# Gathered neighbour rows: slots filled in order of place, blanked by twos two gathers ahead, and their maximum taken two pairs later

## The chip, the cores and the metric

The kernel runs on one core of one Trainium2 chip. The metric is the device time in microseconds (us), the median of three runs. The core has a matrix engine (PE), a vector engine (DVE), a scalar engine (ACT), a general one (POOL, also called GpSimd) and a queue for transfers (SP). They run their own instruction lists and meet only at semaphores.

## The reference

A graph has N = 4096 nodes with 128 features each, `x`, and an adjacency matrix `adj` of 4096 x 4096 with about 16 ones in each row. Two layers follow one another:

```
neighbour_max[i] = max over j with adj[i, j] != 0 of x[j]      (0 without neighbours)
x1 = layernorm(x + neighbour_max)

h  = x1 @ W
e  = leaky_relu((h @ a_src)[:, None] + (h @ a_dst)[None, :], slope 0.2)
att = softmax(e over the valid neighbours); entries under 1e-4 become 0; times the row's degree
out = layernorm(x1 + elu(h + att @ h))
```

The change is in the first layer, the maximum over neighbours.

## The kernel before

**The first layer** goes over eight groups of 512 rows (four tiles of 128), and in each group over 16 pairs of segments (a segment is 128 columns of `adj`). PE turns the adjacency (`turn`, L1027), ranks its ones (`rank`, L1037), and picks for each row and segment one neighbour by a matrix product with `x` split in three bf16 parts (`select`, L1056). DVE folds each pair's result into a running maximum (`best`, L1457). So one neighbour of each segment is dealt with by PE. ACT evicts between them (L785, L792).

**What PE can't take.** If a row has several neighbours in one segment, the others are found by codes and put on a list. DVE works on the list of group g-1 while group g is being selected: `top_keys` at pairs 0, 1, 3, 5, `decode` at pairs 6 and 7, `make_lists` at pairs 8 and 9. The list has up to 15 entries a row. The first five (`DIRECT`) of every row are gathered straight from `x` by row number; for the rows that have more, ten further gathers (`EXTRA`) fetch rows that are later routed to their place by a matrix product.

**The gathers** are POOL's. `G` has 32 slots of 128 partitions x 128 features. A group uses 30 of them: 20 for direct rows (5 entries x 4 tiles) and 10 for extra ones. A list entry that is empty points out of bounds, and its gather writes nothing; so each slot is first blanked with a very small number. POOL's own list of instructions for one group reads: load quarters 0 and 1 of the next group's adjacency (L647, each waits until PE has turned what stood there), blank slot 0, then gathers 0 to 9, each followed by the blank for the next one, load quarter 2, gathers 10 to 19, load quarter 3, gathers 20 to 29. Gather n waits until blank n is complete (`blanked`). The direct gathers (L704) also wait for `list_ready` from `make_lists` (L1547), the extra ones (L712) for the list of extras that DVE writes at pair 12. The blanks are at L696.

**Who takes the rows.** `direct_max` on DVE waits for all 20 direct gathers of group g-2 and folds 20 slots to 4 in three steps (L1582, L1585, L1589): the first step at pair 2 of group g, the two others at pair 4. `extra_rows` at pair 10 waits for the ten extra gathers and folds them (L1597 to L1604); PE routes the result (`route`, L1092) at pair 11, `aggregate` and `normalise` end the layer at pairs 12 to 15. PE's product `heads` (L1146) stands behind pair 4. The first group whose rows are folded this way inside the loop is group 0, during group 2.

**The end of the first layer** overlaps the second. The second layer runs over parts of 4 to 6 segments in a fixed order (`ORDER`): ACT makes the weights of a part (L873), DVE masks them by the adjacency (L1704), PE multiplies (L1246). ACT and DVE may be up to four parts ahead of PE. What is left of the first layer is done between these parts: `direct_max` of groups 6 and 7 behind parts 2 and 12, `extra_rows` of them at 5 and 14, `make_lists` of group 7 at part 3.

Of the kernel before, what the change touches and what calls it, by code (L numbers as in the profile page):

```python
# [15 lines left out]
GT = 4  # L16
# [53 lines left out]
DIRECT = 5  # L70
# [93 lines left out]
def build(nc, x, adj, W, a, out, adjT, x1_all, h_all, d_all, v_all):  # L164
    with ExitStack() as ctx:
# [473 lines left out]
        @block.gpsimd  # L639
        def _(pool):  # L640
            def load_adj(g, k):

                if g >= GROUPS:
                    return
                if g:
                    pool.wait_ge(turned, (g - 1) * PAIRS + (k + 1) * QPAIRS)
                pool.dma_start(adj_in[:, k, :, :], adj_g[g][:, :, k * QUARTER * SEG:(k + 1) * QUARTER * SEG]  # L647
                               ).then_inc(adj_loaded[k], 16)

            half = QUARTER * SEG // 2  # L650

            def load_first(k):

                c = k * QUARTER * SEG
                pool.dma_start(adj_in[:, k, :, 0:half], adj_g[0][:, :, c:c + half]).then_inc(adj_first[k], 16)

            def load_second(k):
                c = k * QUARTER * SEG
                pool.dma_start(adj_in[:, k, :, half:2 * half], adj_g[0][:, :, c + half:c + 2 * half]
                               ).then_inc(adj_loaded[k], 16)  # L660

            load_first(0)
            pool.iota(before[:, :], [[-1, P]], base=0, channel_multiplier=1,
                      allow_small_or_imprecise_dtypes=True).then_inc(consts_pool, 1)
            pool.iota(part_id[:, :], [[0, 1]], base=0, channel_multiplier=1,
                      allow_small_or_imprecise_dtypes=True).then_inc(consts_pool, 1)
            pool.iota(code_val[:, :], [[-BLOCK, BLOCKS - 1]], base=0, channel_multiplier=1,
                      allow_small_or_imprecise_dtypes=True).then_inc(consts_pool, 1)
            pool.iota(block_id[:, :], [[1, BLOCKS]], base=0, channel_multiplier=0,
                      allow_small_or_imprecise_dtypes=True).then_inc(consts_pool, 1)  # L670
            pool.iota(seg16[:, :, :], [[16, SEGS], [0, BLOCKS]], base=0, channel_multiplier=0,
                      allow_small_or_imprecise_dtypes=True).then_inc(consts_pool, 1)
            pool.iota(place_iota[:, :], [[1, P]], base=1 - P, channel_multiplier=0,
                      allow_small_or_imprecise_dtypes=True).then_inc(consts_pool, 1)
            pool.iota(row_id[:, :], [[P, TILES]], base=0, channel_multiplier=1,
                      allow_small_or_imprecise_dtypes=True).then_inc(consts_pool, 1)
            load_second(0)
            pool.wait_ge(consts_pool, 7)
            pool.memset(xs[96:P, QUARTER:SEGS, :], ABSENT).then_inc(x_blank[1], 1)

            for k in range(1, QUARTERS):
                pool.wait_ge(adj_first[k - 1], 16)
                load_first(k)
                pool.wait_ge(adj_loaded[k - 1], 16)
                load_second(k)

            SLOT_AT = [k * GT + t for t in range(GT) for k in range(DIRECT)] + [DIRECT * GT + k for k in range(EXTRA)]

            def blank(g, n):
                if g and n == 0:
                    pool.wait_ge(direct_read, g)
                if g and n == DIRECT * GT:
                    pool.wait_ge(extra_ready, g)
                pool.memset(G[:, SLOT_AT[n], :], ABSENT).then_inc(blanked, 1)  # L696

            def gather(g, n):
                pool.wait_ge(blanked, g * len(SLOT_AT) + n + 1)
                if n < DIRECT * GT:  # L700
                    t, k = n // DIRECT, n % DIRECT
                    if n == 0:
                        pool.wait_ge(list_ready, g + 1)
                    pool.indirect_dma_start(  # L704
                        out=G[:, SLOT_AT[n], :], out_offset=None, in_=x,
                        in_offset=bass.IndirectOffsetOnAxis(ap=idx[:, t, k:k + 1], axis=0),
                        bounds_check=N - 1, oob_is_err=False).then_inc(gathered, 16)
                else:
                    k = n - DIRECT * GT
                    if k == 0:  # L710
                        wait_taken(pool, "index", g + 1)
                    pool.indirect_dma_start(  # L712
                        out=G[:, SLOT_AT[n], :], out_offset=None, in_=x,
                        in_offset=bass.IndirectOffsetOnAxis(ap=idx_extra[:, k:k + 1], axis=0),
                        bounds_check=N - 1, oob_is_err=False).then_inc(extra_gathered, 16)
                if n + 1 < len(SLOT_AT):
                    blank(g, n + 1)

            for g in range(GROUPS + 1):
                load_adj(g + 1, 0)  # L720
                load_adj(g + 1, 1)
                if g:
                    blank(g - 1, 0)
                    for n in range(DIRECT * GT // 2):
                        gather(g - 1, n)
                load_adj(g + 1, 2)
                if g:
                    for n in range(DIRECT * GT // 2, DIRECT * GT):
                        gather(g - 1, n)
                load_adj(g + 1, 3)  # L730
                if g:
                    for n in range(DIRECT * GT, len(SLOT_AT)):
                        gather(g - 1, n)


            pool.wait_ge(ex_listed, 1)
            for c in range(QUARTERS):
                pool.indirect_dma_start(  # L738
                    out=ex_adj[:, c * QUARTER * SEG:(c + 1) * QUARTER * SEG], out_offset=None,
                    in_=adj_q, in_offset=bass.IndirectOffsetOnAxis(ap=exact_idx[:, c:c + 1], axis=0)).then_inc(ex_loaded[c], 16)  # L740
            pool.wait_ge(ex_listed, 2)
            pool.wait_ge(x1_stored, 16 * GROUPS)
            pool.indirect_dma_start(
                out=ex_x1, out_offset=None, in_=x1_all,
                in_offset=bass.IndirectOffsetOnAxis(ap=exact_idx[:, QUARTERS:QUARTERS + 1], axis=0)).then_inc(ex_rows, 16)

            pool.wait_ge(ex_out_ready, 1)
            pool.wait_ge(out_stored[0], 16 * (GROUPS // 2))
            pool.wait_ge(out_stored[1], 16 * (GROUPS // 2))
            pool.indirect_dma_start(  # L750
                out=out, out_offset=bass.IndirectOffsetOnAxis(ap=exact_idx[:, QUARTERS + 1:QUARTERS + 2], axis=0),
                in_=ex_out, in_offset=None, bounds_check=N - 1, oob_is_err=False).then_inc(ex_stored, 16)
            pool.wait_ge(ex_stored, 16)
# [619 lines left out]
        def _(dve):  # L1373
# [341 lines left out]
            for g in range(GROUPS):  # L1715
                for u in range(PAIRS):
# [3 lines left out]
                    if g >= 1:  # L1720
                        if u in (0, 1, 3, 5):
                            top_keys(g - 1, (u + 1) // 2)
                        if u in (2, 4) and g >= 2:
                            direct_max(g - 2, u // 2 - 1)
                        if u in (6, 7):
                            decode(g - 1, u - 6)
                        if u in (8, 9):
                            make_lists(g - 1, u - 8)
                        if u == 10 and g >= 2:
                            extra_rows(g - 2)  # L1730
                        if u == 11 and g >= 2:
                            take_route(g - 2)
                        if u == 11:
                            place_extras(g - 1)
                        if u == 12 and g >= 2:
                            aggregate(g - 2)
                        if u == 12:
                            list_extras(g - 1)
                            if g >= 2:
                                add_own(g - 2)  # L1740
                        if u == 13 and g >= 2:
                            sums(g - 2)
                        if u == (14 if g < GROUPS - 1 else 5):
                            count(g - 1)
                        if g == GROUPS - 1 and u in (14, 15):
                            mask_piece(0, u - 14)
                        if u == 15 and g >= 2:
                            normalise(g - 2)
# [432 lines left out]
```

## Time and profile before

| | us |
|---|---|
| median of 3 runs | 856.14 (855.97 to 856.28) |
| the profiled execution | 856.39 |
| its span, first to last instruction | 854.6 |
| busy in the span: PE | 681.6 |
| DVE | 581.6 |
| ACT | 579.7 |
| POOL | 359.0 |

One execution was recorded by the hardware profiler. Busy is the time in which an engine executed instructions; issuing a transfer from SP, waiting on a semaphore and branching don't count. The granted clock of PE was 0.896 of full speed over the span. POOL's gathers are shown for the time in which POOL makes their descriptors, not for that of the transfer. The stage of the first layer goes from about 10 to 505 us, the gathers from 92 to 616 us.

### The profile page before, as it was taken

The numbers are of one execution on the slowest core, as the hardware profiler recorded it, in microseconds if no ns is written. First come the engines' busy times: TensorE is split into PE (matmuls) and PEld (weight loads), VectorE is DVE, ScalarE is ACT, GpSimd is POOL, SyncE is SP. The second block draws the span as 40 slices with busy tenths as digits, with TensorE's granted clock in tenths as the row PEclk, the third lists the DMA queues.
The fourth block names the chain that finished last, engine by engine and source line by source line (L and its number), as shares of the span: only waits on it lengthen the run. The fifth ranks groups of instructions, "written<-read, shape, count | busy, mean of one in ns | idle before, by whom it ended". The sixth has DMA issues, their size and how long they took to land.

```text
span 854.6 us, 17555 instructions
## 1 busy us (share of the span) xinstructions
PE 681.6 (80%) x6675; PEld 518.7 (61%) x6675; DVE 581.6 (68%) x1320; ACT 579.7 (68%) x853; POOL 359.0 (42%) x534
## 2 busy tenths in 40 slices
PE   3999976966966967966966859799498989899843
PEld 1656643634634634634644439698398888899842
DVE  4657646836836836836846679883374999999683
ACT  4998773754754754754763787689137999998461
POOL 4100466666666666666566566766500000000020
PEclk9999996987987987987996969999699999999957
DMA  9997353743743843743744142231022122322030
GB/s 191 208 181 150 91 120 59 177 109 84 177 108 82 179 106 82 176 108 81 176 106 102 42 161 66 72 113 39 25 86 76 56 81 81 118 81 57 13 53 15
DMA packets 60513, 87.38 MB, mean 102 GB/s; under 512 B 7714, under 2 KB 33326, under 8 KB 60428
## 3 DMA queue, kind: packets, MB, share of 16 engines
q0 software_dynamic: 27328, 42.14, 27.4%
q1 hardware_dynamic: 33100, 44.10, 16.0%
q8 instruction: 55, 0.90, 0.4%
q14 instruction: 30, 0.25, 0.1%
HBM read 108.12 MB, written 21.04 MB: 151 GB/s over the span
## 4 chain that ended last, share of the span: by engine, by line
POOL 35%; issue 24%; PE 16%; DVE 11%; ACT 11%; DMA 1%; POOLq 1%; DVEq 0%; ACTq 0%
POOL G L704 20%; POOL G L712 8%; POOL G L696 6%; PE psR L1246 4%; PE psS L1056 4%; ACT x_split L873 3%; ACT adj_in L873 2%; DVE x_split L1704 2%; ACT at_home L785 2%; PE psA L1027 2%; ACT hot L792 1%; PE psR L1037 1%; PE psR L1331 1%; POOL adj_in L647 1%; DVE acc L1457 1%
## 5 line engine op out<-in xcount | busy, mean ns | idle before, releaser
L704 POOL DMA_INDIRECT G<-in_x_dram,idx x160 | 174.0, 1087 | 139.1 <-POOL G L696 95.2
L1056 PE MATMUL psS<-hot,x_split 128*128 128x512 bf16 x768 | 217.5, 393 | 15.4 <-DVE acc L1457 12.6
L1457 DVE TENSOR_TENSOR acc<-acc,psS 128x1024 f32<-128x1024 f32 x120 | 146.0, 1217 | 66.7 <-PE psS L1056 63.4
L792 ACT ACTIVATE hot<-psR,is_none 128x512 bf16<-128x512 f32 x256 | 166.5, 703 | 19.9 <-PE psR L1037 18.9
L785 ACT ACTIVATE at_home<-psA 128x1024 fp8e4<-128x1024 bf16 x128 | 133.2, 1041 | 58.9 <-PE psA L1027 55.9
L1056 PEld LDWEIGHTS psS<-hot,x_split 128*128 128x128 bf16 x768 | 75.2, 99 | 82.9 <-DVE acc L1457 15.7
L712 POOL DMA_INDIRECT G<-in_x_dram,idx_extra x80 | 92.3, 1154 | 60.6 <-POOL G L696 47.7
L1037 PE MATMUL psR<-at_home,first 128*128 128x512 fp8e4 x256 | 100.6, 394 | 3.4 <-ACT hot L792 3.3
L1071 PEld LDWEIGHTS psC<-taken_book,hot 128*128 128x128 bf16 x1024 | 61.7, 98 | 63.2 <-issue 13.4
L1027 PE MATMUL psA<-ident_bf,adj_in 128*128 128x128 bf16 x1024 | 82.1, 225 | 14.0 <-DVE taken_book L1432 10.6
L738 POOL DMA_INDIRECT adj_in<-in_adj_dram,exact_idx x4 | 5.1, 1282 | 203.7 <-DVE exact_idx L1991 202.8
L1582 DVE TENSOR_TENSOR G<-G 128x1024 f32<-128x1024 f32 x8 | 9.8, 1224 | 112.7 <-DMA G<-in_x_dram,idx 112.7
L1704 DVE SCALAR_TENSOR_TENSOR x_split<-x_split,at_home 128x1024 f32<-128x1024 f32 (+2 forms) x36 | 72.7, 2049 | 11.7 <-ACT x_split L873 11.6
L1027 PEld LDWEIGHTS psA<-ident_bf,adj_in 128*128 128x128 bf16 x1024 | 63.9, 101 | 20.5 <-DVE taken_book L1432 10.6
L1704 DVE SCALAR_TENSOR_TENSOR adj_in<-adj_in,at_home 128x1024 f32<-128x1024 f32 (+2 forms) x40 | 73.2, 1860 | 1.9 <-ACT adj_in L873 1.9
L1146 PE MATMUL psS<-w_aug,x1T 128*128 128x133 f32 x64 | 13.9, 384 | 70.9 <-DVE acc L1457 70.9
L1071 PE MATMUL psC<-taken_book,hot 128*128 128x13 bf16 x1024 | 64.1, 170 | 0.0
L873 ACT ACTIVATE x_split<-acc,minus,r_col 128x512 f32<-128x512 f32 x72 | 51.8, 800 | 17.6 <-PE psC L1246 17.6
L819 ACT COPY h_seg<-psS 128x266 f32<-128x266 f32 x16 | 5.3, 382 | 85.9 <-PE psS L1146 85.9
L1075 PE MATMUL psC<-codebook,at_home 128*128 128x13 bf16 x1024 | 62.5, 168 | 0.0
L873 ACT ACTIVATE adj_in<-rho,minus,r_col 128x512 f32<-128x512 f32 x72 | 52.2, 803 | 10.0 <-PE psC L1246 9.9
L1146 PEld LDWEIGHTS psS<-w_aug,x1T 128*128 128x128 f32 x64 | 12.1, 278 | 71.3 <-DVE acc L1457 71.3
(316 smaller groups left out, 1381.8 us busy)
## 6 DMA issues: line engine op xcount, KB each, us to landing
adj_in<-in_adj_dram POOLq DMA_DIRECT2D x28, 1024.0 KB
adjT_dram<-at_home SPq DMA_DIRECT2D x32, 512.0 KB
at_home<-adjT_dram SPq DMA_DIRECT2D x32, 384.0 KB
adj_in<-in_adj_dram POOLq DMA_DIRECT2D x8, 512.0 KB, 7.7
at_home<-adjT_dram SPq DMA_DIRECT2D x16, 256.0 KB
G<-in_x_dram,idx POOLq DMA_INDIRECT x160
own<-in_x_dram SPq DMA_DIRECT2D x8, 256.0 KB
x_dram<-x1w SPq DMA_DIRECT2D x8, 256.0 KB
```

The lines of the kernel that those rows point to most:

```text
L704: pool.indirect_dma_start(out=G[:, SLOT_AT[n], :], out_offset=None, in_=x, in_offset=bass.IndirectOffsetOnAxis(ap=idx[:, t, k:k + 1], axis=0),
L712: pool.indirect_dma_start(out=G[:, SLOT_AT[n], :], out_offset=None, in_=x, in_offset=bass.IndirectOffsetOnAxis(ap=idx_extra[:, k:k + 1], a ...
L785: nc.scalar.copy(at[:, 2 * u:2 * u + 2, :], turn_home, saturate=True).then_inc(at_ready, 1)
L792: nc.scalar.activation(hot[:, n % 4, :], psR[:, n % 2, :], ACT.Relu, bias=is_none[:, :]).then_inc(hot_ready, 1)
L873: nc.scalar.activation(home[:, s - s0, :], rho[g % 4], ACT.Relu, bias=minus1[:, :], scale=r_col[:, s:s + 1]).then_inc(relu_ready, 1)
L1027: mm = nc.tensor.transpose(turn_home[:, i, t * P:(t + 1) * P], adj_in[:, k, t, at_col:at_col + SEG], ident_bf[:, :])
L1037: nc.tensor.matmul(psR[:, n % 2, :], first[:, :], at[:, n % SEGS, :], start=True, stop=True).then_inc(ranked, 1)
L1056: mm = nc.tensor.matmul(psS[:, b, s % 2 * ROWS:(s % 2 + 1) * ROWS], x_split[:, k, s, :], hot[:, n % 4, :], start=(k == 0), stop=(k == 2))
L1071: mm = nc.tensor.matmul(code_home[:, t, j, :], hot[:, n % 4, t * P:(t + 1) * P], taken_book[:, :], start=False, stop=False, skip_group_che ...
L1075: mm = nc.tensor.matmul(code_home[:, t, j, :], at[:, s, t * P:(t + 1) * P], codebook[:, :], start=False, stop=True, skip_group_check=True)
L1457: V.tensor_tensor(acc_flat, acc_flat, psS[:, b, :], ALU.max).then_inc(free[b], 1)
L1704: mask = V.scalar_tensor_tensor(out=home[:, s0:s1, :], in0=home[:, s0:s1, :], scalar=1.0, in1=ring[:, s0:s1, :], op0=ALU.add, op1=ALU.mult)
```

## The change

Three things. The slots are now filled in their order in memory: gather n fills slot n, so the list entry k is the outer index and the tile t the inner one (before, the other way around). One memset blanks two neighbouring slots, n and n + 1, and is issued behind the even gather n - 2 and not behind the gather just ahead. And `direct_max` does its first step at pair 4 and the rest at pair 6 of a group, where before it was pairs 2 and 4; behind the group loop it stays where it was.

```diff
-            SLOT_AT = [k * GT + t for t in range(GT) for k in range(DIRECT)] + [DIRECT * GT + k for k in range(EXTRA)]
-
-            def blank(g, n):
+            GATHERS = DIRECT * GT + EXTRA
+
+            def blank_two(g, n):
                 if g and n == 0:
                     pool.wait_ge(direct_read, g)
                 if g and n == DIRECT * GT:
                     pool.wait_ge(extra_ready, g)
-                pool.memset(G[:, SLOT_AT[n], :], ABSENT).then_inc(blanked, 1)
+                pool.memset(G[:, n:n + 2, :], ABSENT).then_inc(blanked, 1)

             def gather(g, n):
-                pool.wait_ge(blanked, g * len(SLOT_AT) + n + 1)
+                pool.wait_ge(blanked, (g * GATHERS + n) // 2 + 1)
                 if n < DIRECT * GT:
-                    t, k = n // DIRECT, n % DIRECT
+                    k, t = n // GT, n % GT
                     if n == 0:
                         pool.wait_ge(list_ready, g + 1)
                     pool.indirect_dma_start(
-                        out=G[:, SLOT_AT[n], :], out_offset=None, in_=x,
+                        out=G[:, n, :], out_offset=None, in_=x,
...
-                if n + 1 < len(SLOT_AT):
-                    blank(g, n + 1)
+                if n % 2 == 0 and n + 2 < GATHERS:
+                    blank_two(g, n + 2)

             for g in range(GROUPS + 1):
                 load_adj(g + 1, 0)
                 load_adj(g + 1, 1)
                 if g:
-                    blank(g - 1, 0)
+                    blank_two(g - 1, 0)
                     for n in range(DIRECT * GT // 2):
                         gather(g - 1, n)
                 load_adj(g + 1, 2)
...
-                        if u in (2, 4) and g >= 2:
-                            direct_max(g - 2, u // 2 - 1)
+                        if u in (4, 6) and g >= 2:
+                            direct_max(g - 2, u // 2 - 2)
```

## Rows read from the trace of the kernel before

**Rows 1.** Page: busy time by engine, and the chain that ended last.

```profile
PE 681.6 (80%) x6675; PEld 518.7 (61%) x6675; DVE 581.6 (68%) x1320; ACT 579.7 (68%) x853; POOL 359.0 (42%) x534
...
POOL 35%; issue 24%; PE 16%; DVE 11%; ACT 11%; DMA 1%; POOLq 1%; DVEq 0%; ACTq 0%
```

**Rows 2.** View of waits, DVE and PE, 92 to 617 us: total, times, longest.

```profile
DVE G L1582 <- DMA G<-in_x_dram,idx: 112.7, 7, 17.5
...
PE psS L1146 <- DVE acc L1457: 70.9, 5, 14.8
```

**Rows 3.** Timeline of POOL: start, us, engine, line, operation, in brackets idle before.

```profile
92.02 1.09 POOL L704 DMA_INDIRECT G<-in_x_dram,idx  x1 [12.35 <-DVE idx L1547]
...
218.78 1.08 POOL L704 DMA_INDIRECT G<-in_x_dram,idx  x1 [0.81 <-POOL G L696]
...
238.74 0.22 POOL L696 MEMSET G<- 128x128 f32 x1
238.89 0.83 POOL L647 DMA_DIRECT2D adj_in<-in_adj_dram  x1
240.02 1.04 POOL L704 DMA_INDIRECT G<-in_x_dram,idx  x1 [0.30 <-issue]
...
282.53 1.07 POOL L704 DMA_INDIRECT G<-in_x_dram,idx  x1 [0.80 <-POOL G L696]
...
475.45 1.00 POOL L704 DMA_INDIRECT G<-in_x_dram,idx  x1 [2.42 <-DVE idx L1547]
```

**Rows 4.** POOL by line: 218 to 282 (two rows), 505 to 542.

```profile
L704 POOL DMA_INDIRECT G<-in_x_dram,idx x20 | 21.0, 1048 | 15.3 <-POOL G L696 11.9 <-issue 3.5
L712 POOL DMA_INDIRECT G<-in_x_dram,idx_extra x10 | 10.3, 1034 | 7.4 <-POOL G L696 5.5 <-issue 1.9
...
L712 POOL DMA_INDIRECT G<-in_x_dram,idx_extra x10 | 16.1, 1606 | 7.9 <-POOL G L696 5.5 <-issue 2.4
```

**Rows 5.** Timeline of DVE in the period from 218 us.

```profile
239.65 1.20 DVE L1457 TENSOR_TENSOR acc<-acc,psS 128x1024 f32<-128x1024 f32 x1
...
242.29 1.20 DVE L1457 TENSOR_TENSOR acc<-acc,psS 128x1024 f32<-128x1024 f32 x1
260.61 1.23 DVE L1582 TENSOR_TENSOR G<-G 128x1024 f32<-128x1024 f32 x1 [17.12 <-DMA G<-in_x_dram,idx]
...
279.36 0.17 DVE L1547 TENSOR_SCALAR idx<-listed 128x20 uint32<-128x20 f32 x1
```

**Rows 6.** View of windows: PE, PEld, DVE, ACT, POOL busy; clock; DMA share; GB/s.

```profile
155.00:218.00 63.00, 47.91 (x537) 30.50 (x535) 39.09 (x100) 36.64 (x57) 40.16 (x64) 0.86 0.56 124
218.00:247.00 29.00, 28.77 (x326) 17.99 (x322) 21.95 (x47) 22.61 (x36) 18.43 (x28) 1.00 0.80 174
263.00:267.00 4.00, 3.98 (x19) 3.17 (x20) 3.83 (x7) 1.62 (x4) 2.42 (x5) 0.50 1.04 198
```

**Rows 7.** Timeline of POOL, second of four indirect loads in a row.

```profile
820.18 0.96 POOL L738 DMA_INDIRECT adj_in<-in_adj_dram,exact_idx  x1 [0.30 <-issue]
```

**Rows 8.** Groups by line and shape: the long memset.

```profile
L679 POOL MEMSET h_seg<- 32x3072 f32 x1 | 2.7, 2653 | 0.0
```

**Rows 9.** Timeline of DVE in group 7, the maximum of direct rows.

```profile
453.51 1.23 DVE L1582 TENSOR_TENSOR G<-G 128x1024 f32<-128x1024 f32 x1 [16.60 <-DMA G<-in_x_dram,idx]
```

**Rows 10.** DVE timeline after the group loop: list 7, and its direct maximum.

```profile
532.89 0.17 DVE L1547 TENSOR_SCALAR idx<-listed 128x20 uint32<-128x20 f32 x1
...
593.71 1.23 DVE L1582 TENSOR_TENSOR G<-G 128x1024 f32<-128x1024 f32 x1 [12.97 <-DMA G<-in_x_dram,idx]
```

**Rows 11.** View of waits, 474 to 660 us.

```profile
DVE G L1597 <- DMA G<-in_x_dram,idx_extra: 17.0, 2, 13.5
...
PE psS L1092 <- DVE extra_max L1604: 16.1, 2, 11.2
...
PE psA L1246 <- DVE adj_in L1704: 3.7, 1, 3.7
```

**Rows 12.** Timeline of PE: the route of the last group.

```profile
619.38 2.05 PE L1092 MATMUL psS<-CT,extra_max 128*128 128x512 f32 x2 [11.18 <-DVE extra_max L1604]
```

More of the change, by code:

```diff
@@ L712, in gather @@
                     pool.indirect_dma_start(
-                        out=G[:, SLOT_AT[n], :], out_offset=None, in_=x,
+                        out=G[:, n, :], out_offset=None, in_=x,
                         in_offset=bass.IndirectOffsetOnAxis(ap=idx_extra[:, k:k + 1], axis=0),
                         bounds_check=N - 1, oob_is_err=False).then_inc(extra_gathered, 16)
-                if n + 1 < len(SLOT_AT):
-                    blank(g, n + 1)
+                if n % 2 == 0 and n + 2 < GATHERS:
+                    blank_two(g, n + 2)
             for g in range(GROUPS + 1):
@@ L731, in _ @@
                 if g:
-                    for n in range(DIRECT * GT, len(SLOT_AT)):
+                    for n in range(DIRECT * GT, GATHERS):
                         gather(g - 1, n)
```

## The prediction

> **What bounds the kernel now.** I read the page first. No engine fills the span: PE is busy for 80% of it, POOL for 42%, and yet the chain that ended last runs over POOL for 35% of the span and over "issue", most of it in front of POOL's gathers, for 24% [rows 1]. So the question is who waits for POOL, and the view of waits answers it. From 92 to 617 us DVE stood 112.7 us in seven waits at L1582 (`direct_max`) for gathered rows, and in PE the same stall shows as 70.9 us at L1146, in five waits for a DVE maximum (L1457) that sat behind L1582 [rows 2]. DVE, PE and ACT are one chain here; when DVE stops, all stop.
>
> Next comes POOL's own row of work. One period, from the first gather of a group to the first of the next, goes from 218.78 to 282.53: 63.75 us [rows 3]. Inside it POOL never waits for another engine. A pair of gather and memset takes 2.02 us: 1.00 gather, 0.22 memset, and 0.79 idle while the gather waits for the memset right before it. Two gathers in a period are different: those behind a load of the adjacency, whose memset is older than the load, start 0.30 after it. 28 gaps of 0.79, two of 0.30, 30 memsets, four loads and 30 gathers of 1.04 on average (31.3 us in all) [rows 4] make the 63.75. The first gathers of groups 0 and 6 stand at 92.02 and 475.45, 383.4 us for six periods [rows 3]: POOL is the bound of this stage.
>
> DVE's rows show where it bites: in one group the maximum after pair 2 begins at 260.61 after 17.12 us idle, 41.83 us after the first gather; from there to `list_ready` (L1547) it is 18.8 us [rows 5]. 41.8 + 18.8 + 0.8 is 61.4, less than 63.75, so the loop through the lists has 2.4 us to spare and POOL's own queue decides. PE is busy for 28.8 of 29 us with the clock at 1.00 (2.4 GHz) ahead of the stall, and when it returns, at 263, it gets 0.50 (1.2 GHz) for 4 us and more [rows 6].
>
> **The change, step by step.**
>
> Gaps. Each memset now blanks two slots and is issued behind an even gather for the pair after next, so every gather but the first finds its blanks done while an earlier gather ran. How long is its gap then? Rows of gathers with nothing to wait for: 0.30, behind a load [rows 3] and, near the end, behind another indirect DMA [rows 7]. 15 of 30 gathers will stand behind a gather or a load like these. The other 14 (not the first) stand behind a memset that they needn't wait for, which the trace does not show. Bounds: 0.30 if the 0.79 is the return way of the wait, 0.79 if it belongs to any gather behind a memset. The row nearest to it is the gather at 240.02: there the memset was complete, and of 0.79 no more than 0.30 was left. I take 0.30. 27 gaps lose 0.49: -13.2 us a period.
>
> The Trainium skill (GPSIMD Engine Reference, Instruction dispatch) says that an instruction's completion holds back only what waits on its semaphore and not the next Pool instruction. By that rule the gather behind a finished wait comes at once and the sum is the 745 below; if it did not hold behind a memset, the sum would be that of rival A. The rows show it only behind loads and gathers.
>
> Memsets. 30 of 0.22 become 15 of 256 columns. The price of 128 more columns: the one long memset wrote 3072 columns (of 32 partitions) in 2.65 us [rows 8], against 0.22 for 128, so 0.11 per 128, and one is 0.33. Bounds 0.22 and 0.44. 6.7 - 4.9 = 1.8 us less. The two loads inside the gathers no longer overlap a memset's end by 0.07 each: +0.2. Sum: -14.8, a period of 48.95 for POOL.
>
> Order of slots. Same 20 direct and 10 extra gathers into the same slots, k outermost instead of t: the DVE maximum waits for all 20 anyway, so it costs nothing. If it could be split by slot this would matter; here it can't.
>
> Direct rows. From the first gather to the maximum, 18 gaps of 0.49 (8.8) and 1.0 of memsets go: 41.8 becomes 32.0.
>
> The maximum two pairs later. It was asked for after pair 2, now after pair 4; one pair is 2.6 us of DVE [rows 5]. It then lies 2 pairs nearer to `list_ready`: 18.8 - 5.2, less some 2.2 for PE's cold return which the short stall doesn't bring, plus 0.9 because pair 6 now holds 1.22 + 1.4 + 0.85 of DVE work against 2.6 of pace: 12.3. The loop over the lists is 32.0 + 12.3 + 0.8 = 45.1 < 48.95: hidden under POOL's own queue by 3.8. `blank_two(g, 0)` still waits for the maximum two pairs and more ahead of the list. The blank of the extra slots now stands ahead of gather 19, which waits with it for `extra_rows` of pair 10; POOL gets there 29 us behind the lists of pair 8, so no wait.
>
> Who is late next? PE without the stall: 63.75 - 14.2 (its idle time for each of the five stalls, 70.9 / 5 [rows 2]) - 2 to 2.5 for the half clock = 47 to 47.6. That is just under 48.95, so POOL keeps the bound with 1 to 2 us of wait at L1582. The adjacency loads keep their places in POOL's queue (SP's queue is not touched) and go out, as now, near pairs 10 and 11; the DMA engines' share rises from 0.56 of 63 us [rows 6] to 0.72 of 49, still under one. The two loops are near each other and the gathers will see more neighbours (in one stretch with DVE full ten of them took 1.61 on average [rows 4]); I add 0.5 a period.
>
> Sum of the stage. Before, from the first gather of group 0 to that of group 6: 383.4. After: five periods of 49.45, then 32.0 to the maximum, and from it to the first gather of group 6, which waits only for its list: 14.5 (now 21.9, from 453.51 [rows 9] to 475.45, less 5.2 and 2.2 as above). Sum 293.8. Gain 89.6.
>
> The tail. From 474 on nothing loads adjacency, and POOL's backlog is felt by DVE as one wait of 13.0 for direct rows [rows 10] and two of 17.0 together for extra ones, and at PE as 16.1 for those two (4.9 and 11.2) and 3.7 for the masks behind the first [rows 11]. PE has up to four parts of weights in store and works on through most of DVE's 30, so only its own 19.8 counts. After: list 7 is out at 532.9 in old time, and DVE comes to the maximum of the direct rows at 580.7, 47.8 later [rows 10]; 20 gathers, at the slow 1.45 of this stage, need 39. The ten extras, 21 more, are done some 60 behind the list. PE asks for their result (`route`) at 619.38 - 11.18 = 608.2 [rows 12], or 599.6 when the earlier waits are gone, which is 66.7 behind list 7. So all these waits go: 19.8, plus 2 for the clock, which falls to half in these waits as in the stage's. Gain 21.8. If the extras came late by more than 6 us, each further us would come back. After the tail PE, ACT and DVE take turns as bound, none fed by POOL.
>
> Total: 856.4 (this execution; its span is 854.6, and the median is 856.1) - 89.6 - 21.8 = 745.0.
>
> **Rivals.**
>
> A, the gap stays behind a memset: 14 gathers keep 0.79. POOL's period is 48.95 + 6.9 = 55.8, five times, and ten of them in the last direct path: 34.3 + 4.9 = 39 later, 784. For it: every 0.79 in the trace is behind a memset. Against: the memset of 240.02. Half way lies 0.46, where the memset's own 0.33 would hide that much of the 0.79: 14 times 0.16 in five periods and 1.6 in the last path are 13 more, 758, inside the likely range.
>
> B, nothing overlaps, since POOL takes a gather up only when idle: all gaps stay, only the memsets shrink, by 1.8 in each of eight groups, 842. Against: the 0.30 rows [rows 3, 7].
>
> C, another loop takes over above 49: PE's turns waiting for adjacency, or DVE's pair 6. At 52 it costs 6 times 3: 763.
>
> D, slower. Gathers stretch beside DVE. In the stretch 505 to 542, with masks L1704 on DVE nearly without pause, ten gathers took 1.61 on average [rows 4]. If the unstalled DVE did this to all 30, the period would be 48.95 + 17.1 = 66.1, 2.3 above now: six of them make 14, and the tail's waits stay: 870. It decides from a mean of 1.53 on (1.04 + 14.8/30). Against: from 218 to 247 DVE is busy for 21.95 of 29 us [rows 6], and the gathers of that group still average 1.04.
>
> The Trainium skill (SBUF — State Buffer, Who interferes with whom) says that a DVE instruction with two SBUF inputs contends with a GpSimd instruction that reads SBUF. L1704 has two such inputs and its neighbours are long here, so the trace agrees; L1457, the DVE work of this stage, reads one from PSUM, so by that rule D does not come about and the sum stays.
>
> **How the numbers follow.** Likeliest 0.69: 745, own range 735 to 762. A 0.15, B 0.04, C 0.08, D 0.03, something unseen that costs all 0.01. The range reaches from 732 (POOL under PE's 47 and a little more in the tail) to 788 to hold A; what is above is B and D. A measurement can tell 0.2% from no change: faster 0.96, same 0.01, slower 0.03.
>
> **What the profile will show.** Gathers at 1.0 with 0.30 before them, also behind memsets; 0.79 there would be A. Memsets 120 of 0.33. Starts of periods 49 apart. The wait at L1582 falls from 17 to 1 to 3 us, PE's at L1146 likewise, PEclk stays 1.0 in the stage. No wait at L1597, L1092 in the tail. If L1582 waits for nothing and PE is full, PE is the bound and the time is nearer 735. I am wrong if gathers lengthen, or if L1027 waits for a load.

## The result, and the profile after

The changed kernel takes 740.33 us, median of four runs (738.39 to 743.35), against 856.06 for the kernel before in the same comparison. The ratio is 0.8652, interval 0.8618 to 0.8686: 13.5% less time. The forecast was 745 in a range of 732 to 788. The profiled execution took 738.39, that is 118.0 less than the profiled one before (856.39), where the prediction's sum had 111.4. The four runs of the changed kernel span 5 us, so of the single runs below only differences well above that are read.

The changed kernel has one line more, so L1582 of before is L1583 here, L1704 is L1705, and POOL's gathers are L705 and L713. First the page: busy time, PE's granted clock over the 40 slices of the span, and the chain that ended last by engine.

```profile
PE 652.0 (89%) x6605; PEld 503.8 (68%) x6675; DVE 580.6 (79%) x1320; ACT 579.0 (79%) x853; POOL 353.0 (48%) x414
...
PEclk9999999999999999999999899998999999999856
...
PE 42%; DVE 27%; ACT 14%; issue 10%; POOL 6%; DMA 0%; POOLq 0%; DVEq 0%; ACTq 0%
```

POOL, 35% of that chain before [rows 1], has 6% of it, and PE has 42%. The clock, which in the kernel before read 0.50 to 0.53 behind each of the six stalls of the stage ([rows 6] shows one), is 1.00 here from 92 to 379 us (windows below).

The timeline of POOL (start, length, idle before in brackets) shows the first gathers of groups 0, 1, 4 and 6, and how gather and memset alternate:

```profile
92.04 1.09 POOL L705 DMA_INDIRECT G<-in_x_dram,idx  x1 [12.24 <-DVE idx L1548]
93.13 0.33 POOL L697 MEMSET G<- 128x256 f32 x1
93.63 1.04 POOL L705 DMA_INDIRECT G<-in_x_dram,idx  x1 [0.17 <-POOL G L697]
94.97 1.00 POOL L705 DMA_INDIRECT G<-in_x_dram,idx  x1 [0.30 <-issue]
...
138.89 1.07 POOL L705 DMA_INDIRECT G<-in_x_dram,idx  x1 [0.80 <-POOL G L697]
...
281.25 1.07 POOL L705 DMA_INDIRECT G<-in_x_dram,idx  x1 [2.47 <-DVE idx L1548]
...
378.95 1.00 POOL L705 DMA_INDIRECT G<-in_x_dram,idx  x1 [5.68 <-DVE idx L1548]
```

The kernel before had, at a gather inside a period:

```profile
235.72 1.00 POOL L704 DMA_INDIRECT G<-in_x_dram,idx  x1 [0.79 <-POOL G L696]
```

Behind a memset whose end the gather need not wait for, 0.17 is left of the 0.79; behind a gather it is 0.30. The first period, 92.04 to 138.89, is 46.85, and its end waits for nothing but POOL's own first blank (0.80). DVE's lists come 47.8 to 47.9 apart from the second on, so POOL, with its 46.85, catches up with them: its first gathers are 46.85, 47.0, 47.5 and then 47.9 apart, and from group 3 on they wait for the list, 0.9 to 2.5 us each and 5.68 in group 6. From 92.04 to 378.95 it is 286.9, where before it was 383.4 [rows 3]: 96.5 of the 118.0.

The view of waits (us in total, times, longest), DVE from 92 to 617 us and PE from 141 to 379:

```profile
DVE acc L1458 <- PE psS L1057: 46.1, 45, 2.2
...
DVE G L1598 <- DMA G<-in_x_dram,idx_extra: 8.3, 1, 8.3
...
PE psS L1093 <- DVE extra_max L1605: 2.8, 5, 0.6
```

The waits of L1582, 112.7 us in seven, and those of L1146, 70.9 us in five [rows 2], are gone from the stage; only one wait of DVE for direct rows is left in the whole span, 5.10 in the tail (below). What DVE waits for is now PE. The windows (PE, PEld, DVE, ACT, POOL busy; clock; DMA share; GB/s) say the same: PE is busy for 276 of 287 us, and for 46.98 of 48 in one period, at clock 1.00, where before it had 0.86 over a period [rows 6]. The first two rows belong to the tail and are read further down.

```profile
377.93:432.84 54.91, 44.36 (x396) 35.42 (x401) 45.99 (x110) 45.08 (x68) 41.10 (x45) 0.94 0.34 104
432.84:501.04 68.20, 62.56 (x550) 61.10 (x548) 52.70 (x81) 57.23 (x84) 56.94 (x44) 0.99 0.27 78
188.00:236.00 48.00, 46.98 (x548) 29.92 (x554) 40.68 (x101) 38.46 (x59) 40.16 (x50) 1.00 0.76 165
92.00:379.00 287.00, 276.32 (x3201) 175.38 (x3254) 237.63 (x590) 228.17 (x337) 231.99 (x293) 1.00 0.72 156
```

### The profile page after: what moved, and what is told of

Its sections match the earlier page's. It is cut to its first block, busy times and chain, and to the rows that moved or that the text cites. A ratio compares the mean times of both kernels' runs of the same rounds, so it can differ in the third digit from the quotient of the medians.

```text
span 736.5 us, 17365 instructions
## 1 busy us (share of the span) xinstructions
PE 652.0 (89%) x6605; PEld 503.8 (68%) x6675; DVE 580.6 (79%) x1320; ACT 579.0 (79%) x853; POOL 353.0 (48%) x414
## 4 chain that ended last, share of the span: by engine, by line
PE 42%; DVE 27%; ACT 14%; issue 10%; POOL 6%; DMA 0%; POOLq 0%; DVEq 0%; ACTq 0%
PE psS L1057 14%; DVE acc L1458 6%; PE psA L1028 5%; PE psR L1038 5%; PE psR L1247 4%; DVE x_split L1705 3%; ACT x_split L874 3%; ACT adj_in L874 3%; POOL G L705 3%; PE psC L1072 2%; PE psC L1076 2%; ACT at_home L786 2%; ACT hot L793 2%; DVE adj_in L1705 2%; POOL G L713 1%
## 5 line engine op out<-in xcount | busy, mean ns | idle before, releaser
L705 POOL DMA_INDIRECT G<-in_x_dram,idx x160 | 183.7, 1148 | 67.9 <-DVE idx L1548 30.7
L1057 PE MATMUL psS<-hot,x_split 128*128 128x512 bf16 x698 | 193.7, 380 | 7.6 <-DVE shift L1659 2.3
L1038 PE MATMUL psR<-at_home,first 128*128 128x512 fp8e4 x256 | 97.4, 381 | 3.4 <-ACT hot L793 3.3
L713 POOL DMA_INDIRECT G<-in_x_dram,idx_extra x80 | 89.2, 1115 | 19.9 <-issue 14.6
L1028 PE MATMUL psA<-ident_bf,adj_in 128*128 128x128 bf16 x1024 | 79.0, 221 | 14.0 <-DVE taken_book L1433 10.4
L1705 DVE SCALAR_TENSOR_TENSOR x_split<-x_split,at_home 128x1024 f32<-128x1024 f32 (+2 forms) x36 | 72.7, 2049 | 11.4 <-ACT x_split L874 11.3
L1028 PEld LDWEIGHTS psA<-ident_bf,adj_in 128*128 128x128 bf16 x1024 | 61.3, 98 | 20.3 <-DVE taken_book L1433 10.4
L1705 DVE SCALAR_TENSOR_TENSOR adj_in<-adj_in,at_home 128x1024 f32<-128x1024 f32 (+2 forms) x40 | 73.2, 1859 | 1.9 <-ACT adj_in L874 1.9
L1072 PE MATMUL psC<-taken_book,hot 128*128 128x13 bf16 x1024 | 63.6, 170 | 0.1
L1247 PE MATMUL psR<-at_home,adj_in 128*128 128x130 f32 x416 | 50.8, 284 | 5.9 <-DVE adj_in L1705 5.9
L1247 PEld LDWEIGHTS psR<-at_home,adj_in 128*128 128x128 f32 x416 | 49.8, 199 | 7.1 <-issue 7.1
L1247 PE MATMUL psR<-at_home,x_split 128*128 128x130 f32 x352 | 42.2, 282 | 3.5 <-DVE G L1784 3.5
L1247 PE MATMUL psS<-at_home,x_split 128*128 128x130 f32 x368 | 44.1, 275 | 0.0
```

The costliest lines, as they stand in the source:

```text
L705: pool.indirect_dma_start(out=G[:, n, :], out_offset=None, in_=x, in_offset=bass.IndirectOffsetOnAxis(ap=idx[:, t, k:k + 1], axis=0), boun ...
L713: pool.indirect_dma_start(out=G[:, n, :], out_offset=None, in_=x, in_offset=bass.IndirectOffsetOnAxis(ap=idx_extra[:, k:k + 1], axis=0), b ...
L1028: mm = nc.tensor.transpose(turn_home[:, i, t * P:(t + 1) * P], adj_in[:, k, t, at_col:at_col + SEG], ident_bf[:, :])
L1038: nc.tensor.matmul(psR[:, n % 2, :], first[:, :], at[:, n % SEGS, :], start=True, stop=True).then_inc(ranked, 1)
L1057: mm = nc.tensor.matmul(psS[:, b, s % 2 * ROWS:(s % 2 + 1) * ROWS], x_split[:, k, s, :], hot[:, n % 4, :], start=(k == 0), stop=(k == 2))
L1072: mm = nc.tensor.matmul(code_home[:, t, j, :], hot[:, n % 4, t * P:(t + 1) * P], taken_book[:, :], start=False, stop=False, skip_group_che ...
```

## The experiments

Each kernel below is one edit of the kernel before or of the changed one. Where an interval is given, the kernel was timed in rounds against the kernel before.

**1. The later maximum alone.** The kernel before with this one edit:

```diff
-                        if u in (2, 4) and g >= 2:
-                            direct_max(g - 2, u // 2 - 1)
+                        if u in (4, 6) and g >= 2:
+                            direct_max(g - 2, u // 2 - 2)
```

> The kernel before with only the maximum of the direct rows at pairs 4 and 6. Theory (the return of the wait on each blank sets POOL's period, and the period sets the stage): POOL's period stays 63.7, the wait at L1582 shrinks to about 12 because it begins two pairs later, and the stage is not faster; only the last list (group 6) waits less, so 851 to 857. Rival (the later maximum is what frees DVE): six periods lose two pairs of 2.6 each, about 825.

Measured 852.3 us, ratio 0.9976 (0.9958 to 0.9993). The view of waits for DVE over the whole span, then two rows of POOL's timeline, the first gathers of groups 1 and 5:

```profile
DVE G L1582 <- DMA G<-in_x_dram,idx: 73.3, 7, 12.9
...
DVE G L1597 <- DMA G<-in_x_dram,idx_extra: 43.6, 7, 13.5
...
155.40 1.09 POOL L704 DMA_INDIRECT G<-in_x_dram,idx  x1 [0.80 <-POOL G L696]
...
409.87 1.08 POOL L704 DMA_INDIRECT G<-in_x_dram,idx  x1 [0.80 <-POOL G L696]
```

Four periods take 254.5, 63.6 each, against 63.9 in the same four groups without the edit. Without the tail's 12.9, L1582 still waits 60.4 in six groups, 10 each and not 17, and 4 to 6 in each of five groups turn up at L1597 (`extra_rows`), which did not wait in the stage before. The greater part of the wait has moved along the queue. So the rival falls: as long as POOL's period is near 63.7, asking later buys 2.5 us in all.

**2. The blanks alone.** The changed kernel with the reverse of that edit, the maximum back at pairs 2 and 4.

> The changed kernel with the maximum back at pairs 2 and 4. Theory: POOL's direct rows are in 31.1 us behind the list, DVE asks for them at pair 2, 28.9 behind it, so it waits about 2.2 in each of six groups: 753 (748 to 756). Rival (with the gaps gone POOL is ahead anyway, the later maximum is worth nothing): 740, the same as the changed kernel.

Measured 748.75 us, ratio 0.8754 (0.8732 to 0.8775), 8.4 more than the changed kernel, whose interval ends at 0.8686. The first gather of group 3, DVE's maximum and list in that period, and the next first gather:

```profile
238.79 1.07 POOL L705 DMA_INDIRECT G<-in_x_dram,idx  x1 [3.21 <-DVE idx L1548]
...
269.52 1.23 DVE L1583 TENSOR_TENSOR G<-G 128x1024 f32<-128x1024 f32 x1 [3.22 <-DMA G<-in_x_dram,idx]
...
287.04 0.17 DVE L1548 TENSOR_SCALAR idx<-listed 128x20 uint32<-128x20 f32 x1
...
288.06 1.07 POOL L705 DMA_INDIRECT G<-in_x_dram,idx  x1 [3.21 <-DVE idx L1548]
```

L1583 waits 3.2 to 4.7 in six groups, 21.5 in all, and the periods are 49.3 and not 47.9. What sets them is neither POOL's own queue nor PE but the loop through the lists: 30.7 from the first gather to the maximum, 17.5 from there to the list, 1.0 to the next first gather. In the changed kernel the middle part is 13.75 (170.79 to 184.54, shown further down), and the loop, 30.3 + 13.75 + 1.0, comes to 45 and is no longer the longest. The later maximum is worth 9.0 us over the six periods (295.9 against 286.9) once POOL is fast, and 2.9 before (383.4 against 380.5, the kernel before and that of experiment 1).

**3. One slot a memset, still two gathers ahead.** The changed kernel with

```diff
-                pool.memset(G[:, n:n + 2, :], ABSENT).then_inc(blanked, 1)
+                pool.memset(G[:, n, :], ABSENT).then_inc(blanked, 1)
...
-                pool.wait_ge(blanked, (g * GATHERS + n) // 2 + 1)
+                pool.wait_ge(blanked, g * GATHERS + n + 1)
...
-                if n % 2 == 0 and n + 2 < GATHERS:
+                if n + 2 < GATHERS:
```

and slots 0 and 1 blanked ahead of the first gather.

> The changed kernel with 30 memsets of one slot instead of 15 of two, each still two gathers ahead. Theory (it is the distance, not the number of memsets): every gather stands 0.17 behind a memset of 0.22, POOL's body is 0.2 to 0.4 shorter or equal, PE stays the bound: 740, within 3. Rival (fewer memsets are what helps): 15 more memsets and gaps of 0.79 or so come back, over 770.

Measured 741.13 us, ratio 0.8675 (0.8651 to 0.8699): no difference from the changed kernel. POOL's timeline:

```profile
145.96 1.00 POOL L705 DMA_INDIRECT G<-in_x_dram,idx  x1 [0.17 <-POOL G L697]
146.96 0.22 POOL L697 MEMSET G<- 128x128 f32 x1
147.34 1.00 POOL L705 DMA_INDIRECT G<-in_x_dram,idx  x1 [0.16 <-POOL G L697]
```

A slot costs 1.00 + 0.22 + 0.16, and two of them 2.76. In the changed kernel a pair costs 2.00 + 0.33 + 0.17 + 0.30, which is 2.80. The memsets saved are paid back by the 0.30 that a gather has behind a gather, against 0.17 behind a memset. So the gain is the distance between blank and gather, not the number of memsets; experiment 4 is the other half of this.

**4. Two slots a memset, right ahead of their gathers.** The changed kernel with

```diff
-                if n % 2 == 0 and n + 2 < GATHERS:
-                    blank_two(g, n + 2)
+                if n % 2 == 1 and n + 1 < GATHERS:
+                    blank_two(g, n + 1)
```

> The changed kernel with the memset of two slots right before the first of its two gathers, as before the change but by twos. Theory: 15 gathers wait 0.79 again and the other 15 have 0.30, POOL's period is 47.0 + 9.3 = 56.3 and it is the bound again: 5 periods of 8.5 more and 5 in the last path, about 787 (780 to 792). Rival (the number of memsets counts): 740.

One run, 787.1 us, 47 more than the changed kernel. POOL's timeline:

```profile
149.68 0.34 POOL L697 MEMSET G<- 128x256 f32 x1
150.80 1.36 POOL L705 DMA_INDIRECT G<-in_x_dram,idx  x1 [0.79 <-POOL G L697]
152.47 1.00 POOL L705 DMA_INDIRECT G<-in_x_dram,idx  x1 [0.30 <-issue]
```

The 0.79 is back before each gather that waits for the memset ahead of it, and only there. The periods are 54.5 (147.28 to 365.29 is four), 1.8 less than expected: behind two of the 14 memsets an adjacency load is issued first, and the gathers behind those wait for nothing. 46.85 with 12 of 0.62 and 2 of 0.13 more is 54.55. The time is the one expected. The memsets are as many as in the changed kernel and as wide; only their place differs.

**5. More work for POOL.** The changed kernel with one more memset of 256 columns, into a tile that nobody reads, ahead of each blank.

> The changed kernel with one more memset of 256 columns into a tile nobody reads behind each of the 15 blanks' places: POOL work of 0.33 each, 5.0 a period. Theory (POOL's 47.0 lies just under PE's 47.85, so the knee is within 1 us): POOL's period becomes 52.0 to 52.4 and is the bound, five periods of 4.3 and 2 to 4 in the last path and tail: 765 (760 to 770). Rival (PE is the bound with room below it): less than 5 more, 745.

One run, 758.76 us. POOL's timeline and DVE's wait for direct rows:

```profile
147.10 0.33 POOL L702 MEMSET dose<- 128x256 f32 x1
147.35 0.33 POOL L704 MEMSET G<- 128x256 f32 x1
147.84 1.00 POOL L712 DMA_INDIRECT G<-in_x_dram,idx  x1 [0.16 <-POOL G L704]
```

```profile
DVE G L1590 <- DMA G<-in_x_dram,idx: 18.3, 7, 5.2
```

POOL is the bound again: periods of 50.4 (142.93 to 344.52 is four), and DVE waits seven times. The dose was smaller than meant. A memset behind a memset starts before the other ends and adds 0.25, not 0.33, so a period has 3.8 more, and 46.85 + 3.8 is 50.6. It costs 2.5 a period over PE's 47.9, where 3.8 were added: POOL has 1 us of room below PE in the changed kernel, no more.

**6. The last group one part later.** In the changed kernel, behind the group loop, `direct_max` and `extra_rows` of the last group on DVE and `route` and `index` on PE each one part later (two of the four shown):

```diff
-                if i == 12:
+                if i == 13:
                     direct_max(GROUPS - 1, 0)
...
-                if i == 13:
+                if i == 14:
                     late("route", GROUPS + 1)
```

> The changed kernel with the last group's direct maximum, extra rows, route and index one part of the second layer later. Theory (the tail's PE wait of 4.8 at the route is the rest of POOL's lateness): PE no longer waits there, 735 to 737. Rival (PE's wait is only moved: the steps behind it come later too and the store of x1 is late): 740 or more.

Measured 738.37 us (734.15 to 739.21), ratio 0.8625 (0.8593 to 0.8657). The interval covers the changed kernel's 0.8652. No gain over the changed kernel is shown, although PE's longest wait at the route fell from 4.80 to 1.3 us. The view of PE's waits from 377 to 520 us shows where most of it went:

```profile
PE psS L1116 <- DVE x1w L1647: 3.0, 1, 3.0
...
PE psS L1093 <- DVE extra_max L1605: 1.7, 2, 1.3
```

PE now waits 3.0 for the normalised rows (`x1w`), a later step, where the changed kernel waits 0.2 at most. That is what the rival says; the median lies between the two forecasts, and the run does not decide between a gain of about 2 us and none.

**7 and 8. What makes a gather long.** In the changed kernel, ahead of the running maximum in pairs 9 to 15, where direct gathers run, DVE does one maximum more that leaves the result as it is; in one kernel of `acc` with itself (both inputs in SBUF), in the other of `acc` with the PSUM region (one input in SBUF):

```diff
+                    if g >= 1 and u >= 9:
+                        after(mark(V.tensor_tensor(acc_flat, acc_flat, acc_flat, ALU.max)))
```

> The changed kernel with an additional maximum of acc with itself (128x1024, both inputs in SBUF, result unchanged) ahead of the running maximum in pairs 9 to 15 of groups 1 to 7, where the direct gathers run. Theory (a DVE instruction with both inputs in SBUF holds up POOL's gathers): direct gathers of groups 1 to 5 rise from 1.01 to 1.03 to 1.2 or more, period 51 to 54. Rival (the long gathers of the tail come from something else): gathers stay at 1.03; the time grows only by DVE's 7 times 1.3 a period less its room of 7, some 2 to 4 a period.

> As dve_two_sbuf, but the additional maximum is that of acc with the psS region (one input in SBUF, one in PSUM), same size and place, result unchanged. Theory: gathers stay at 1.01 to 1.04, shorter than in dve_two_sbuf. Rival: both alike.

One run each, 790.18 and 785.75 us. First the kernel with two SBUF inputs, one gather of POOL and the additional maximum of DVE, then the same of the kernel with one:

```profile
101.36 1.86 POOL L705 DMA_INDIRECT G<-in_x_dram,idx  x1 [0.16 <-POOL G L697]
...
101.12 1.23 DVE L1459 TENSOR_TENSOR acc<-acc 128x1024 f32<-128x1024 f32 x1 [2.34 <-PE psS L1057]
```

```profile
102.38 1.00 POOL L705 DMA_INDIRECT G<-in_x_dram,idx  x1 [0.16 <-POOL G L697]
...
102.38 1.22 DVE L1459 TENSOR_TENSOR acc<-acc,psS 128x1024 f32<-128x1024 f32 x1 [1.75 <-PE psS L1057]
```

The gather at 101.36 lies under a DVE maximum that begins at 101.12 and is 1.86 long; the one at 102.38 in the second kernel begins with such a maximum and is 1.00. Over the 100 direct gathers of groups 1 to 5 the mean is 1.229 with two inputs in SBUF and 1.055 with one, 1.018 in the changed kernel; 41 of the 100 are longer than 1.2 us with two, nine with one. So both inputs in SBUF is what counts. What one input adds is small: other kernels here without the added instruction have means up to 1.03. Both kernels' periods (55.9 and 54.6) are above what I expected, 51 to 54. The added maxima are 8.5 us a period and cost 8.3 and 7.0 over the changed kernel's 47.6 in the same groups, so DVE's idle time of 7 us a period was no room for them. In both kernels the first gathers of groups 2 to 5 start 5 to 7 us after POOL is free, when DVE's list is there, so the longer gathers do not set the period. The reason why DVE could not use its idle time was not tested.

**9. The order of the slots.** Experiment 3 with the tile outermost as before the change: the old `SLOT_AT` for the slot, and `t, k = n // DIRECT, n % DIRECT`.

> As one_slot_each, but the slots in the order from before the change (tile outermost, list entry inner). Theory (DVE waits for all 20 direct rows, so the order is free): 741, within 3 of one_slot_each. Rival (filling the slots in order of place is part of the gain): 750 or more.

Measured 881.12 us, ratio 1.0279 (1.0261 to 1.0296), which neither side had expected. The slow place is PE: its timeline has idle time inside a run of small products, and the view of waits (95 to 370 us) finds nothing that PE waited for ("issue"):

```profile
120.28 0.23 PE L1078 MATMUL psC<-codebook,at_home 128*128 128x13 bf16 x3 [1.23 <-issue]
...
PE psA L1030 <- issue: 16.2, 13, 3.3
```

PE's idle time of this kind from 95 to 370 us sums to 37 us; in the changed kernel it is none. The granted clock in this stretch is 0.86, against 1.00. The idle time is no scatter: DVE's waits behind it, 5.36, 3.84 and 1.85 at 189.80, 200.16 and 204.76, come again as 5.26, 3.86 and 1.85 at 257.91, 268.33 and 272.93, one period later. The kernel that ran next to it on the same chip showed such idle time too:

**10. Two of three parts in `select`.** The lowest bf16 part of `x` left out of the products (`range(2)`), so the neighbour maxima are less exact.

> The changed kernel with select multiplying by two of the three bf16 parts of x (the lowest part left out, so the maxima are less exact): 32 matrix products of 0.21 less in each group, 6.8 of PE's 47.9. Theory (POOL's queue lies 1 us under PE): the first gathers of groups 1 to 5 come 47.0 apart and no closer, so in that stretch the 6.8 are nearly worthless; what is saved is before the first gather and after the last list, 10 to 25 in all: 715 to 730. Rival (PE alone bounds the stage): starts 41 to 42 apart, 690 or less.

One run, 844.76 us, with 24 us of such idle time on PE. It can't be compared with anything. It was to show by less work on PE that PE is the bound of the stage; that rests on PE's busy share and on experiment 5 instead.

**11 and 12. The same again.** Both on one chip: the changed kernel unchanged, and the kernel of experiment 9 unchanged.

> The changed kernel itself, beside order_again on one chip. If the 881 of order_tile_outer and the 845 of select_two_of_three came from the chip that they ran on (there PE shows idle time with nothing waited for, 37 and 24 us from 95 to 370, where all other kernels show 2 or less), this one too may be at 845 to 885; if they came from the kernels, it is 740.

> order_tile_outer unchanged, beside changed_again. If the order of the slots is what slows PE's supply of instructions: 881 again with changed_again at 740. If it was the chip or its state: the two are alike, 740 each or both far above.

Measured 740.52 us, ratio 0.8658 (0.8643 to 0.8672), and 739.0 us, ratio 0.8638 (0.8612 to 0.8663). The same kernel that took 881 takes 739 here, and its PE has no idle time without a cause from 95 to 370. So the order alone does not make the 881, and in the runs that compare it undisturbed (739.0 beside 740.52) the order of the slots is free, as predicted. What held PE back in experiments 9 and 10 is open: all five runs of experiment 9 took 879 to 889, the kernel before ran beside them at 856.82, as elsewhere, and experiments 5 to 8 had run on the chip of the same number without such idle time. A chip that is slow at everything is not the answer either.

## Why the prediction was right

**What bounds.** Right. POOL's period of 63.75 set the stage, and the 0.79 between the end of a blank and the gather that waits for it set POOL's period. Experiment 4 puts that wait back before 12 of the 30 gathers and changes little else, and costs 47 us. Experiment 1 moves DVE's wait and leaves POOL's queue, and gains 2.5.

**The gap behind a memset**, bounded by 0.30 and 0.79 and taken as 0.30, is 0.17: below the range. 14 of 0.13 make 1.8 a period. The bound from below was the error. I took the 0.30 behind a load or a gather for the least that a gather can have, and it is what stands behind those two only. The rule weighed there (the Trainium skill, GPSIMD Engine Reference, Instruction dispatch: completion holds back only what waits on the semaphore) agrees with the 0.17.

**The memset** of 256 columns: 0.33 predicted, 0.33 measured.

**The direct rows and the list.** From the first gather to the last direct one plus landing, 32.0 was forecast; the twentieth gather starts 27.9 behind the first (138.89 to 166.79), and with the 2.4 of before it would be 30.3. DVE comes later than that. Its timeline, the maximum and list of one group, then the list of group 7 and what it waits for in the tail:

```profile
170.79 1.22 DVE L1583 TENSOR_TENSOR G<-G 128x1024 f32<-128x1024 f32 x1
...
184.54 0.16 DVE L1548 TENSOR_SCALAR idx<-listed 128x20 uint32<-128x20 f32 x1
...
432.84 0.17 DVE L1548 TENSOR_SCALAR idx<-listed 128x20 uint32<-128x20 f32 x1
...
480.56 1.23 DVE L1583 TENSOR_TENSOR G<-G 128x1024 f32<-128x1024 f32 x1 [5.10 <-DMA G<-in_x_dram,idx]
...
498.84 0.82 DVE L1598 TENSOR_TENSOR G<-G 128x640 f32<-128x640 f32 x1 [8.32 <-DMA G<-in_x_dram,idx_extra]
```

The maximum at 170.79 waits for nothing. It was to wait 1 to 3. From there to the list it is 13.75, where I had 12.3 for a group inside the stage. Experiment 1, where DVE stood 10 us ahead of the same maximum, has 12.4. This fits a DVE that goes at PE's pace in the changed kernel and, after a stall, finds PE's results ready; the sum had no term for that.

**Who is late next.** PE, at 47 to 47.6, was to be just under POOL's 48.95 + 0.5. It is just over: 47.9 against 46.85. The term that was mis-sized is POOL's period, 49.45 in the sum: 1.8 of the difference is the gap, 0.5 the addition for gathers among more neighbours, which did not come, as the direct gathers of groups 1 to 5 average 1.02, and 0.3 is left over. The forecast for the stage was a gain of 89.6, measured is 96.5. This hides a second error of the other sign: the first five periods take 237.1 and not 247.3, but from the first gather of group 5 to that of group 6 it is 49.8 where the sum had 46.5 (33.1 to the maximum and not 32.0, then 16.8 to the first gather and not 14.5). Rival C expected another loop to take over above 49; PE takes over at 47.9, which is below the period forecast for POOL.

**The tail** was to give 21.8, and it gave 21.5 (the span of the tail from the first gather of group 6: 380.9 before, 359.4 after, each with what lies around the span), but not in the way that was written, so this agreement is luck. That no wait would be left is wrong: DVE still waits 5.10 for the direct rows and 8.32 for the extra ones, and PE waits at the route, as its timeline shows:

```profile
443.57 1.13 PE L1093 MATMUL psS<-CT,extra_max 128*128 128x512 f32 x2 [0.84 <-DVE extra_max L1605]
...
501.04 2.05 PE L1093 MATMUL psS<-CT,extra_max 128*128 128x512 f32 x2 [4.80 <-DVE extra_max L1605]
```

4.80 where there were 11.18 [rows 12], and 0.84 where the kernel before had 4.87:

```profile
547.16 1.80 PE L1092 MATMUL psS<-CT,extra_max 128*128 128x512 f32 x2 [4.87 <-DVE extra_max L1604]
```

The gathers are the greater part of the reason. I priced them at 1.45 in the tail; here is POOL by line from 432 to 505 us:

```profile
L705 POOL DMA_INDIRECT G<-in_x_dram,idx x20 | 37.6, 1882 | 11.3 <-DVE idx L1548 6.9 <-issue 2.7 <-POOL G L697 1.6
L713 POOL DMA_INDIRECT G<-in_x_dram,idx_extra x10 | 14.7, 1474 | 2.5 <-issue 1.8 <-POOL G L697 0.7
```

The direct ones average 1.88, which makes 20 of them 8.6 longer. The rest is that DVE and PE come for them sooner than the sum had it: DVE asks for the direct rows 42.6 behind the list and not 47.8, since 5 us of its own waits in that stretch went too, and PE for the route 63.4 behind it and not 66.7. The gather that took longest lies under two rows of masks back to back, both inputs in SBUF (POOL first, then DVE):

```profile
469.23 7.11 POOL L705 DMA_INDIRECT G<-in_x_dram,idx  x1 [0.17 <-POOL G L697]
...
468.58 3.48 DVE L1705 SCALAR_TENSOR_TENSOR x_split<-x_split,at_home 128x1024 f32<-128x1024 f32 x3
471.98 3.48 DVE L1705 SCALAR_TENSOR_TENSOR adj_in<-adj_in,at_home 128x1024 f32<-128x1024 f32 x3
```

7.11 us, from 469.23 to 476.34, under masks from 468.58 to 475.46. Experiments 7 and 8 show that a DVE instruction with both inputs in SBUF lengthens gathers; that it is the whole of the 7.11 was not tested. The clock made up for the waits. The windows of the kernel before, from the list of group 6 to that of group 7 and on to the route, show 0.85 and 0.90:

```profile
474.43:532.89 58.46, 48.93 (x408) 36.87 (x409) 46.44 (x110) 46.45 (x70) 36.90 (x54) 0.85 0.30 98
532.89:619.38 86.49, 66.60 (x541) 64.11 (x540) 52.80 (x81) 56.43 (x83) 56.42 (x66) 0.90 0.20 62
```

The changed kernel has 0.94 and 0.99 there (windows above), and the two stretches are 3.5 and 18.3 shorter. PE's idle time of 19.8 at the route and masks fell to 5.6, which is 14.1; the rest, 7.7, goes with the higher clock (PE's busy time in the two stretches falls from 115.5 to 106.9), on which I had put 2. In the first of the two stretches PE is not less idle than before (10.6 against 9.5), and it is still 3.5 shorter.

**The rivals.** A (the gap stays behind a memset) and B (nothing overlaps) are refuted by the 0.17. D, gathers made long by DVE, does not happen in the stage but does in the tail, and experiment 7 brings longer gathers into the stage: 1.23 with one added instruction of two SBUF inputs in each of seven pairs. The mean of 1.53 from which D was to decide was not reached in the stage even so.

The page of the Trainium skill that I weighed for D (SBUF — State Buffer, Who interferes with whom) says that a DVE instruction with two SBUF inputs contends with a GpSimd instruction that reads SBUF; experiments 7 and 8 agree, 1.23 against 1.05.

## What to carry to other kernels

A wait on the instruction right ahead, on the same engine, can cost more than that instruction (here 0.6 us more than without the wait, 28 times in a period, behind a memset of 0.22 us), so issue what is waited for one work item earlier and expect nothing from merging the small ones. Move a wait only when the queue behind it is no longer the bound: the later maximum brought 2.5 us before the blanks moved and 8.4 after (medians). When the bound of a stage falls, work out every other loop to within 1 us, since here the next one stood that near, and the sum hangs on which of them is longer.

## What the runs showed of the hardware

- On POOL a gather starts 0.17 us behind a memset that it need not wait for, 0.30 behind a gather or a load, and 0.79 behind a memset whose semaphore it waits for.
- A memset takes 0.22 us for 128 columns of fp32, 0.33 for 256, and one of 256 adds 0.25 when it follows another of 256 directly.
- The making of a gather's descriptors, 1.00 us alone, is lengthened beside DVE instructions with both inputs in SBUF: 1.9 beside a single one, a mean of 1.23 against 1.05 over 100 gathers. One gather took 7.1 under two rows of such masks back to back.
- Two kernels on one chip showed idle time of PE that nothing in the profile explains (37 and 24 us from 95 to 370 us, 881 and 845 us in all); one of them, unchanged, took 739 on another chip. The cause is open.
